# Gates of every second expert pair brought by DMA in an attention and mixture-of-experts kernel

## The reference, cut to what matters

```python
x = x + xattn(layernorm(x), ctx, ctx, ...)      # 16 heads of 8, causal softmax; 8 batches of 256 tokens of 128
# then the feed-forward part, per token, on xt = layernorm(x)
up_s = einsum('th,seh->tse', xt, shared_up)                 # 2 shared experts of 64
shared = einsum('tse,she->th', gelu(up_s), shared_down)
probs = softmax(xt @ router_w.T)                            # 16 routed experts
topk_p, topk_i = top_k(probs, 4)
gate = zeros_like(probs).at[rows, topk_i].add(topk_p)       # 0 for the 12 experts not chosen
up_r = einsum('th,reh->tre', xt, routed_up)
act = gelu(up_r) * gate[:, :, None]
routed = einsum('tre,rhe->th', act, routed_down)
return x + shared + routed
```

## Time and profile before

| | us |
|---|---|
| median of 3 runs | 219.24 (218.1 to 220.63) |
| the profiled execution | 219.43 |
| its span in the profile | 217.7 |
| PE busy | 187.0 (86%) |
| DVE busy | 170.6 (78%) |
| ACT busy | 143.4 (66%) |
| POOL busy | 97.1 (45%) |

### The profile page before, as it was taken

One profiled execution on the slowest core, in us unless ns is written; L12 is line 12 of the kernel. 1 busy time (PEld: TensorE's weight loads), 2 busy tenths in 40 slices (PEclk: granted clock), 3 DMA queues, 4 the chain that ended last, 5 costly groups with the idle time before them and its releaser, 6 DMA issues.

```text
span 217.7 us, 4911 instructions
## 1 busy us (share of the span) xinstructions
PE 187.0 (86%) x1610; PEld 137.3 (63%) x1610; DVE 170.6 (78%) x456; ACT 143.4 (66%) x285; POOL 97.1 (45%) x184
## 2 busy tenths in 40 slices
PE   0538689959999899999999997879959989999992
PEld 0316465646777577677767774457848758787871
DVE  4589969829689989999899994237788597787881
ACT  2261267746697687776766778866868977668661
POOL 5789018929569666566474666711112000000000
PEclk9999999996999999999999999999999999999999
DMA  4524332651332312312313200100000010010011
GB/s 121 168 62 121 77 102 78 212 155 52 93 87 51 103 56 63 106 39 77 79 53 81 74 5 5 32 6 24 3 2 0 5 50 0 0 48 0 9 41 48
DMA packets 23736, 12.98 MB, mean 60 GB/s; under 512 B 4696, under 2 KB 23400, under 8 KB 23712
## 3 DMA queue, kind: packets, MB, share of 16 engines
q1 hardware_dynamic: 23040, 12.52, 20.9%
q10 hardware_dynamic: 576, 0.13, 0.3%
q0 software_dynamic: 96, 0.03, 0.1%
HBM read 3.86 MB, written 1.05 MB: 23 GB/s over the span
## 4 chain that ended last, share of the span: by engine, by line
PE 50%; DVE 20%; issue 9%; SPq 8%; ACT 6%; DMA 3%; POOL 2%; POOLq 0%; DVEq 0%; ACTq 0%
DVE sb_mx L774 8%; SPq L335 6%; PE psum L964 6%; PE psum L946 4%; PE psum L883 3%; PE psum L880 3%; PE psum L881 3%; PE psum L923 3%; PE psum L865 3%; PE psum L867 3%; PE psum L866 3%; DVE sb_qk_res L757 2%; PE psum L872 2%; PE psum L967 2%; PE psum L930 2%
## 5 line engine op out<-in xcount | busy, mean ns | idle before, releaser
L774 DVE TENSOR_REDUCE sb_mx<-psum 128x2 f32<-128x512 f32 (+1 forms) x96 | 63.0, 679 | 8.0 <-PE psum L930 5.3
L582 ACT ACTIVATE sb_probs<-psum 128x512 f32<-128x512 f32 x96 | 55.9, 603 | 18.9 <-PE psum L946 18.0
L428 POOL TENSOR_SCALAR_AFFINE_SELECT sb_probs<-sb_probs 128x256 f32<-128x256 f32 (+1 forms) x96 | 45.1, 484 | 35.0 <-ACT sb_probs L582 34.4
L665 DVE TENSOR_TENSOR sb_probs<-sb_probs,psum 128x512 f32<-128x512 f32 x32 | 21.9, 684 | 10.1 <-ACT sb_probs L526 9.8
L526 ACT ACTIVATE sb_probs<-psum 128x512 f32<-128x512 f32 x36 | 21.4, 599 | 12.1 <-PE psum L867 12.0
L946 PE MATMUL psum<-sb_qk_op 128*128 128x256 bf16 x128 | 24.6, 274 | 3.1 <-ACT sb_probs L582 3.0
L923 PE MATMUL psum<-sb_qk_op 96*128 96x256 bf16 x128 | 25.9, 285 | 0.0
L672 DVE TENSOR_TENSOR sb_hid_l<-sb_probs,sb_hid_h 128x512 fp32r<-128x512 f32 x36 | 24.7, 685 | 0.3
L532 ACT CAST sb_hid_h<-sb_probs 128x512 fp32r<-128x512 f32 x36 | 22.2, 616 | 2.9 <-DVE sb_probs L665 2.9
L920 PE MATMUL psum<-sb_fut,sb_id_b 128*128 128x256 bf16 x64 | 18.3, 286 | 5.2 <-issue 4.4
L964 PE MATMUL psum<-sb_probs,sb_v_op 128*32 128x256 f32 x256 | 20.9, 398 | 0.8 <-ACT sb_o_raw L557 0.8
(11 more groups left out here) (114 smaller groups left out, 391.1 us busy)
## 6 DMA issues: line engine op xcount, KB each, us to landing
sb_qk_op<-sb_qk SPq DMA_DIRECT2D x96, 64.0 KB
sb_ctx<-in_ctx_t SPq DMA_DIRECT2D x8, 128.0 KB, 2.4
sb_num<-sb_o_raw SPq DMA_DIRECT2D x8, 128.0 KB, 2.1
out<-sb_o_raw SPq DMA_DIRECT2D x4, 256.0 KB, 2.3
sb_x<-in_x SPq DMA_DIRECT2D x3, 256.0 KB, 4.1
sb_up_f<-in_rup_t SPq DMA_DIRECT2D x1, 512.0 KB, 3.6
sb_dn_f<-in_rdown SPq DMA_DIRECT2D x1, 512.0 KB, 4.5
sb_x<-in_x SPq DMA_DIRECT2D x2, 128.0 KB, 3.5
```

Of the source, the lines that this page charges most:

```text
L428: nc.gpsimd.affine_select(out=v, in_=v, compare_op=ALU.is_ge, fill=0.0, base=0, pattern=[[0, v.shape[1]], [1, P]], channel_multiplier=-1). ...
L582: nc.scalar.activation(probs[g][:, u * BANK:(u + 1) * BANK], psum[:, BANK_S + n % SB, :], ACT.Exp, scale=float(DH) ** -0.5).then_inc(s_exp, 1)
L665: nc.vector.tensor_tensor(hid[buf[k]], gel[buf[k]], psum[:, 3 + k % 2, :], ALU.mult)\
L774: nc.vector.tensor_reduce(dst, src, AX, ALU.max).then_inc(m_max, 1)
```

## The change

The eight experts of chunks k=2, 4, 6 and 8 no longer get their gates by a matmul. POOL writes their gates eight times side by side into `g_parts` (two more copies per batch), so that PE's transposition of `g_parts` leaves each expert's gates on eight partitions; ACT copies the transposed bank once more as float32 to `gate_f` (the free tile `xn`), ahead of `gate_t`. SP then issues eight DMAs for every tile of 512 tokens (`load_gates`), each of which reads eight partitions of `gate_f`, each of them eight times, and writes 64 partitions of `gates`, which lies in the free operand buffer `qk_op[0]`. `gated` of an even chunk multiplies by that SBUF tile. Tiles 0 and 1 are issued at the end of SP's turn 9, tiles 2 and 3 after turn 11. PE's line 872 runs only for odd k, its bank wait is three chunks back in place of one, and `early_units` has 18 chunks: three in turn 9 (t = 8, 9, 10), six in turn 10 at t = 1, 2, 5, 7, 9, 10 (before 1, 2, 4, 6, 8, 10), nine in turn 11 as before.

```diff
+        gate_f = xn[:, :, :].rearrange("p a e -> p (a e)")
+        gates = qk_op[0][:, :, :, :].rearrange("p h n s -> p (h n s)").bitcast(F32).rearrange("p (i q) -> p i q", q=BANK)
+        REPS = 8
-        early_units = ((8, 10), (1, 2, 4, 6, 8, 10), (0, 1, 2, 4, 6, 7, 8, 9, 10))
+        early_units = ((8, 9, 10), (1, 2, 5, 7, 9, 10), (0, 1, 2, 4, 6, 7, 8, 9, 10))
...
+            def load_gates(n):
+                sp.wait_ge(gf_read, BANK // S * (n + 1))
+                sp.wait_ge(s_ps, UNITS * (NB - 1))
+                sp.wait_ge(hid_done, NCH * max(n - 1, 0))
+                for i in range(4):
+                    for h in range(2):
+                        rows = gate_f[32 + 32 * h + i:64 + 32 * h:4, n * BANK:(n + 1) * BANK]
+                        sp.dma_start(gates[h * P // 2:(h + 1) * P // 2, 4 * (n % 2) + i, :],
+                                     rows.unsqueeze(1).to_broadcast([REPS, P // 2 // REPS, BANK]))\
+                            .then_inc(gates_in[4 * (n % 2) + i], 16)
...
+                if turn.at == NB + 1:
+                    load_gates(0)
+                    load_gates(1)
...
-            with sp.Fori(0, NCT) as n:
+            for n in range(NCT):
+                if n + 2 < NCT:
+                    load_gates(n + 2)
                 sp.wait_ge(y_done, n + 2)
...
+                        for h in range(2):
+                            copies = g_parts[:, :, 2 + 2 * h:4 + 2 * h, :].bitcast(F32).rearrange("p a n r -> p a (n r)")
+                            nc.gpsimd.tensor_copy(copies.rearrange("p a (n r) -> p a n r", r=4),
+                                                  gate[:, :, 2 + h:NR:4].unsqueeze(2).to_broadcast([P, QB, REPS, 4]))\
+                                .then_inc(g_last, 1)
...
                         act.wait_ge(gt_ps, count(c + 1))
+                        nc.scalar.copy(gate_f[:, c * S:(c + 1) * S], psum[:, BANK_A, 0:S]).then_inc(gf_read, 1)
                         nc.scalar.copy(gate_t[:, bass.ds(c * S, S)], psum[:, BANK_A, 0:S])\
                             .then_inc(gt_read, 1)
...
+                elif k % 2:
+                    dve.wait_ge(gate_ps, NCH // 2 * n + k // 2 + 1)
+                    nc.vector.tensor_tensor(hid[buf[k]], gel[buf[k]], psum[:, 3 + k // 2 % 2, :], ALU.mult)\
+                        .then_inc(hid_done, 1)
                 else:
-                    dve.wait_ge(gate_ps, (NCH - 1) * n + k)
-                    nc.vector.tensor_tensor(hid[buf[k]], gel[buf[k]], psum[:, 3 + k % 2, :], ALU.mult)\
-                        .then_inc(hid_done, 1)
+                    i = 4 * (n % 2) + k // 2 - 1
+                    dve.wait_ge(gates_in[i], 32 * (n // 2 + 1))
+                    nc.vector.tensor_tensor(hid[buf[k]], gel[buf[k]], gates[:, i, :], ALU.mult).then_inc(hid_done, 1)
...
-                if k > 0:
+                if k % 2:
-                    pe.wait_ge(hid_done, count(at - 1) if isinstance(at, int) else at - 1)
-                    mm(psum[:, 3 + k % 2, :], spr[:, P * (k - 1):P * k], gate_t[:, cols], start=True, stop=True).then_inc(gate_ps, 1)
+                    pe.wait_ge(hid_done, count(at - 3))
+                    mm(psum[:, 3 + k // 2 % 2, :], spr[:, P * (k - 1):P * k], gate_t[:, cols], start=True, stop=True)\
+                        .then_inc(gate_ps, 1)
...
-                        pe.wait_ge(g_last, count(c + 1))
+                        pe.wait_ge(g_last, 3 * (c + 1))
```

9 lines of the change are left out of this document (5 added, 4 removed).

## The result

The changed kernel took 227.48 us (226.98 to 228.1, 4 runs), the kernel before, run beside it, 219.94 us: a ratio of 1.036, 95% interval 1.031 to 1.041. I had predicted 220.6, with 223.2 as the upper end: wrong, by 6.9 us. In the table further down a median counts every execution and a ratio leaves out the slow ones, those more than 1.5% above the fastest of their kernel (one of e5's, one of e14's and seven of e11's ten).

What follows compares the result with a forecast made beforehand. PE's instruction count was taken to bound the last stage, a serial chain turns 9 and 10. Parts two to four +3.5, part one -2.3, POOL 0.2: +1.4 on 219.43, less 0.2 for the median, 220.6 us; range 216.4 to 223.2.

Steps and rivals of the forecast that it cites:

- turns 4 to 8: Turns 4 to 8: ACT's additional copy fits in its slack; zero, at worst 0.2 us in each of five turns.
- Part one: Last stage: 15 fewer matmuls save 3.5 us, 1.0 and 0.2 are lost again; -2.3 us.
- Part two: Turn 9: the third chunk puts `gated` and `low` ahead of the residual on DVE; +1.2 us.
- Part three: Turn 10: displaced chunk makes `att` 1.3 us later; with two chunks ahead, the residual comes 2.4 us later.
- Part four: Turn 11: PE idles 2.1 us ahead of chunk (1, 3); the gates' transposition comes 3.5 us later.
- the near row: POOL's two new copies in turn 11, priced like its existing ones at 0.29 us spacing; cost 0.6 us.
- The DMAs: Gate copies ahead of `den`: a full queue moves 257 GB/s, so `den` is in time; zero.
- rival (b): Turn 10: `den` late if gate copies run at 155 GB/s or less; at 128 GB/s +2.8, 223.4 us; 12%.
- POOL and DVE: Turns 9 to 11: POOL's rstd held up by DVE instructions with two SBUF inputs; 0.2 us added.
- (a): PE's work is the time after all, turn 11's waits don't come; 217.4 us, or 216.1; 17%.
- (d): The DMAs replace nothing on the path and the new places cancel out; 219.2 us; 8%.
- (c): POOL's copies are dear, reaching PE in turns 4 to 8 from about 0.6 us each; +2.5, 223 us; 13%.

Runs made afterwards that it cites:

- e5: Changed kernel with TensorE's wait for ACT's reading of xn2 in turn 11 moved behind the seven matmuls of chunk (1, 3); 223.16 us, ratio 1.013.
- e14: e7 with the edits of e11 and e12, plus matmuls nobody reads in TensorE's waits of turns 10 and 11; 218.48 us, ratio 0.992.
- e11: e7 with gate_t copied ahead of gate_f on ACT; 220.61 us, ratio 0.992.
- e3: Changed kernel with 27 added matmuls nobody reads, in TensorE's waits of turns 10 and 11 and ahead of tile 2; 223.16 us, ratio 1.014.
- e9: e2 with TensorE's wait for ACT's reading of xn2 in turn 11 moved behind chunk (1, 3)'s seven matmuls; 221.25 us, ratio 1.004.
- e6: Changed kernel with tile 1's eight gate DMAs issued at the end of turn 10, behind `den`; 225.72 us, ratio 1.026.
- e2: Kernel before with only the new places of the early chunks, gates still by matmul; 222.70 us, ratio 1.012.
- e8: e2 with eight matmuls nobody reads in TensorE's two waits of turn 10; 222.71 us, ratio 1.010.
- e16: Kernel before with six, nine and two matmuls nobody reads in TensorE's waits of turns 9 to 11; 219.27 us, ratio 0.999.
- e15: e10 with 20 matmuls nobody reads in TensorE's waits of turns 10 and 11 and ahead of tile 2; 221.37 us, ratio 1.007.
- e12: e7 with the last batch's eightfold gate copies made by ACT in place of POOL; 220.46 us, ratio 1.001.
- e7: e1 with tile 1's gate DMAs issued at the end of turn 10; 220.89 us, ratio 1.004.
- e1: Changed kernel with the early chunks put back in their old places, gates still by DMA; 222.55 us, ratio 1.012.
- e10: Changed kernel with the edits of both e5 and e6; 223.85 us, ratio 1.014.

## Why the prediction was wrong

**The step that failed** is one that I never wrote down as a step: in every part I priced a wait of PE at its own length and every matmul at 0.233 us. From turn 9 on the profile before gave no reason to doubt it, with a clock of 1.00 there and in the earlier trace rows, in spite of waits of 2.19 us. But I had looked no further: at 49 to 53 us the same profile has a wait of 2.24 us and matmuls at half clock behind it. The changed kernel has more waits in its last turns, and three stretches of 3.7 to 3.9 us at about half clock follow. By e3 they cost 3.6 us in the two stretches. The Trainium skill describes such a thing in "TensorE: Matmul & The Clock Gate", section "HAM oscillation — how this bites in real kernels": there waits for DMAs between bursts of matmuls let the clock fall, so that the next burst starts slow. The trace agrees in kind, with waits of 1.1 to 2 us for ACT, DVE and POOL; but the same waits were also followed by no fall (e5, e9 in turn 10, e6 in turn 11).

The two stretches were forecast at +1.2 us and came to +7.6. Of the 6.4 us between, 3.6 are the clock (e3). Some 2.1 are in the turns at full clock (e3: +5.6, forecast +3.5) and 0.8 in the last stage (e3: -1.5, forecast -2.3). They are terms that had the wrong size, named below part by part. A further 0.4 us lies ahead of turn 9, in turns 4 to 8, which I had put at zero: from the projection at 58.44 us to turn 9's router it takes 81.3 us in every kernel without the gate path (before, e2, e8, e9, e16) and 81.6 to 81.7 in every kernel with it.

**Part one** forecast -2.3 us for the last stage, and it was +0.2. The terms were nearly right: the start of tile 2 came 1.57 us after the transposition (1.2 forecast), and with the clock held the stage is 1.5 us shorter than before (e3). Of the 0.8 that is missing, 0.4 is that start and 0.3 that a tile takes 14.4 us and not 14.1: the profile of after shows 195.70 to 210.08 for one tile, with a short stop of PE ahead of the last chunk's matmuls down (0.52 us from one start to the next at 208.75, against 0.29 before), which I had left out. The rest, 1.65 us, is the slow matmuls behind the transposition.

**Part two**, the residual of turn 9: 149.25 instead of 147.51, 1.7 us later; the turn itself had begun 0.4 us later, so 1.3 against the 1.2 forecast. Right.

**Part three**, turn 10: the exponential at 158.32 (157.2), the output projection at 163.07 (161.8), the residual at 165.40 (164.0). 1.1 to 1.4 us too little, of which 0.4 is the turn's later start. The order of events is as forecast; there is a wait of 1.17 us for `den`, which I had excluded and which costs 0.2 (e3 against e15) to 0.5 us (e6), and the displaced chunk's matmuls ran at half clock, for 0.2 us (e3).

**Part four**, turn 11: the stop of PE in front of chunk (1, 3), for ACT's reading of xn2, is there with 1.84 us (2.1 forecast), and with the fall behind it it is the dearest single piece of the change, 3.1 us (e5). It came 0.6 us later after the start of the turn than I had it (7.3 against 6.7 us from turn 10's transposition of the gates to its end). From there to the chunk of t=6 it took 4.1 us (171.04 to 175.15) and not 2.4: the slow matmuls, for e6, with the same stop and no fall, has 2.5. And from there to the gates' transposition 10.9 us, not 10.0, for POOL's two copies took 1.50 us at the spot where I had 0.6 by the near row.

**The DMAs** were the second failed step. I divided 72 GB/s by their share of 0.28 and took all engines to be busy: the gates' copies run at 144 GB/s at a share of 0.53. That makes 272 GB/s for a full share, so the price of a busy engine was about right, and what was wrong is that all of them would be busy. The Trainium skill ("DMA: Bandwidth & Descriptors", section "Rules for kernel authors") has the rule that I missed: the slowest dimension of a copy sets how many engines it uses, and here that is the 8 partitions read. The share of 0.53, about half of 16, agrees with it; no run here copies the gates in another shape. This is rival (b), whose threshold I had put at 155 GB/s and its chance at 12%. At 144 GB/s `den` cost 1.17 us in DVE's wait, and 0.5 us of turns 9 and 10 by e6.

**POOL and DVE** sharing SBUF: I had added 0.2 us. It shows in the pair of copies, 0.52 against 1.50 us, and in rstd's second instruction, 0.72 us in turn 10's start and 1.02 in turn 11's. The Trainium skill ("SBUF — State Buffer", section "SBUF: two separate sides") says that a POOL instruction that reads SBUF and a DVE instruction with two inputs there exclude one another for the whole instruction; the trace agrees with it in kind, and e12 shows that the path hardly felt the pair: with the copies on ACT, turn 11 is 0.4 us shorter than e7's.

**The rivals.** (a) and (d) are refuted by the result, and by e1 and e2, where each half of the change costs time by itself. Of (b) the sign came, a wait for `den` of over 1 us, but not its price of 2.8 us in this kernel; e1 against e7, with the old places, has it at 2.2. (c) happened only in turn 11. What none of them had is the clock. Not settled are the 2.3 to 3.9 us by which the turns of e9 and e15 are longer at full clock: I take them for the chunks ahead of the residuals (parts two and three forecast 2.4 at the residual of turn 10) and, in e15, for the gate path besides (e1: turn 11 0.8 us longer), but no run took one chunk away alone. Not settled either is what makes a fall follow one wait and not another. It came or stayed away behind waits of the same length, in identical code (e2 and e9 in turn 10) and between kernels (after and e6 in turn 11), so a difference between single profiles, such as e5 against e10, can be that.
